# A first stage that runs from a table of ranks: a newly searched table, with new duration figures and new filler matmuls

## The reference, cut to what matters

```python
x = x + _L0_xattn_ref(_layernorm(x), pos, ..., ctx_1024, ...)   # the first stage
x = x + _L0_ffn_ref(_layernorm(x), w1, mean_w1, w2, mean_w2, w3, mean_w3)
```

```python
def _binary_diff_weight(w, base):
    d = w - base
    coeff = jnp.mean(jnp.abs(d))
    return base + coeff * jnp.sign(d)
```

## Time and profile before

| | |
|---|---|
| median of 3 runs | 1187.7 us (1187.0 to 1189.63) |
| the profiled execution, its own time | 1188.86 us |
| its span, first to last instruction | 1187.1 us |
| PE, share of the span | 97% (1157.4 us) |
| DVE, ACT, POOL | 77%, 60%, 39% |
| 0 to 50 us: PE, DVE, ACT busy | 41.91, 38.48, 37.41 us |
| 40 to 360 us: PE, DVE, ACT busy | 303.74, 254.33, 249.23 us |
| 360 to 1187 us: PE, DVE, ACT busy | 820.75, 632.18, 437.06 us |
| granted PE clock, mean of the span | 0.995 |

### The profile page before, as it was taken

One profiled execution on the slowest core, in us unless ns is written; L12 is line 12 of the kernel. 1 busy time (PEld: TensorE's weight loads), 2 busy tenths in 40 slices (PEclk: granted clock), 3 DMA queues, 4 the chain that ended last, 5 costly groups with the idle time before them and its releaser, 6 DMA issues.

```text
span 1187.1 us, 17254 instructions
## 1 busy us (share of the span) xinstructions
PE 1157.4 (97%) x6191; PEld 907.8 (76%) x6191; DVE 917.0 (77%) x1241; ACT 714.0 (60%) x1019; POOL 466.2 (39%) x593
## 2 busy tenths in 40 slices
PE   7998999999999999999999999999999999999998
PEld 5764666667677888888787888888888888888887
DVE  7866688788999788877798678766875777888764
ACT  6878679868686765656556556565663343333342
POOL 3778878886632542435433433354230000000000
PEclk9999999999999999999999999999999999999999
DMA  9677676663513577668766775768667978752232
GB/s 331 222 272 273 232 277 239 256 245 103 178 54 113 180 274 206 216 212 268 235 179 209 267 243 195 241 215 275 200 200 249 344 244 284 258 188 102 94 133 97
DMA packets 99160, 255.39 MB, mean 215 GB/s; under 512 B 9458, under 2 KB 24068, under 8 KB 98820
## 3 DMA queue, kind: packets, MB, share of 16 engines
q1 hardware_dynamic: 95044, 239.62, 56.5%
q0 software_dynamic: 4032, 14.68, 6.9%
HBM read 212.85 MB, written 41.42 MB: 214 GB/s over the span
## 4 chain that ended last, share of the span: by engine, by line
PE 81%; DVE 10%; ACT 4%; issue 3%; DMA 1%; POOL 1%; SPq 0%; DVEq 0%; ACTq 0%; POOLq 0%
PE pair L1590 30%; PE quad L1590 12%; PE quad L1637 11%; PE pair L1637 11%; PE quad L1524 2%; PE quad L1534 2%; PE pair L1571 2%; PE pair L1693 2%; PE pair L1496 1%; DVE negwide L2214 1%; ACT prob L1854 1%; PE pair L1461 1%; PE pair L1476 1%; PE pair L1423 1%; PE quad L1527 1%
## 5 line engine op out<-in xcount | busy, mean ns | idle before, releaser
L2592 POOL TENSOR_TENSOR raw_w<-raw_w,raw_base 128x256 f32<-128x256 f32 x224 | 195.0, 933 | 165.0 <-DMA raw_base<-in_mean_w 165.0
L2125 ACT ACTIVATE split<-grid 128x1024 fp32r<-128x1024 f32 x98 | 104.0, 1061 | 159.8 <-PE pair L1637 147.9
L2534 DVE TENSOR_TENSOR split<-grid,split 128x1024 fp32r<-128x1024 f32 x98 | 119.7, 1224 | 62.1 <-ACT split L2125 61.8
L1637 PE MATMUL quad<-split 128*128 128x512 f32 x588 | 149.3, 389 | 0.5 <-DVE hid L2541 0.5
L1637 PE MATMUL pair<-split 128*128 128x512 f32 x588 | 149.2, 389 | 0.0
L1637 PEld LDWEIGHTS quad<-split 128*128 128x128 f32 x588 | 110.3, 188 | 23.7 <-DVE split L2534 0.9
L1637 PEld LDWEIGHTS pair<-split 128*128 128x128 f32 x588 | 110.4, 188 | 22.9
L1590 PE MATMUL pair<-t_b_hi,ring_hi 128*128 128x512 f32 x224 | 89.0, 397 | 2.5 <-ACT snap L2089 1.8
L2306 DVE TENSOR_TENSOR ring_lo<-raw_base,ring_hi 128x1024 fp32r<-128x1024 f32 x56 | 72.4, 1293 | 22.0 <-ACT ring_hi L2073 14.3
L1590 PE MATMUL pair<-t_b_lo,ring_hi 128*128 128x512 f32 x224 | 88.4, 395 | 0.0
L1590 PE MATMUL pair<-t_b_hi,ring_lo 128*128 128x512 f32 x224 | 87.6, 391 | 0.0
(11 more groups left out here) (328 smaller groups left out, 2801.8 us busy)
## 6 DMA issues: line engine op xcount, KB each, us to landing
raw_w<-in_w SPq DMA_DIRECT2D x56, 512.0 KB, 5.7
raw_base<-in_mean_w SPq DMA_DIRECT2D x56, 512.0 KB, 7.6
grid<-h_blocks SPq DMA_DIRECT2D x49, 512.0 KB, 3.7
late<-in_mean_w SPq DMA_DIRECT2D x28, 512.0 KB, 5.8
late<-in_w POOLq DMA_DIRECT2D x28, 512.0 KB, 5.6
grid<-in_mean_w SPq DMA_DIRECT2D x28, 512.0 KB, 4.8
h_blocks<-work SPq DMA_DIRECT2D x42, 256.0 KB, 3.0
ctxw<-in_w SPq DMA_DIRECT2D x20, 512.0 KB, 4.1
```

Of the source, the lines that this page charges most:

```text
L1637: a = pe.matmul(into[t], found[:, a, t * P:(t + 1) * P], found[:, b, :], start=p == 0 and n == 0 and q < 4, stop=p == PAIRS - 1 and n == 2 ...
L2125: act.activation(splits[n % RINGS][:, 0:2, :], operands(n), ACT.Copy).then_inc(a_hi, 1)
L2534: dve.tensor_tensor(found[:, 2:4, :], operands(n), found[:, 0:2, :].bitcast(F32), ALU.subtract).then_inc(a_lo, 1)
L2592: a = pool.tensor_tensor(w[:, some], w[:, some], base[:, some], ALU.subtract)
```

## The change

It replaces three tables, and no function. `WORK` gets some other figures, `RANK` is replaced as a whole (1019 ranks), `LULLS` has other entries (52 filler matmuls in place of 51). No arithmetic, buffer, DMA or wait of a step is changed; what changes is the order of each engine's list, the banks that steps get, and where the fillers stand.

```diff
-RAT = [... ("DVE", 1.72, 0.2), ("ACT", 0.83), ("DVE", 2.83, 0.25), ("POOL", 2.05), ("POOL", 0.64), ("DVE", 2.2, 2.2)]
+RAT = [... ("DVE", 1.66, 0.2), ("ACT", 0.83), ("DVE", 2.82, 0.25), ("POOL", 1.75), ("POOL", 0.64), ("DVE", 2.42, 2.42)]
...
-    ("measure", 0): (2, 17, 5, 70, 88, 103, ...
+    ("measure", 0): (48, 55, 39, 60, 70, 78, ...
...
-    ('front', 0, 11): (1, 0, ('front', 0, 11)),
+    ('turnmax', 1, 0): (1, 7, ('turnmax', 1, 0)),
-    ('fill', 13, 0): (1, 4, ('turnmax', 5, 0)),
+    ('back', 1, 4): (1, 4, ('weigh', 14, 0)),
-    ('fill', 17, 0): (1, 6, ('weigh', 14, 0)),
+    ('fill', 17, 0): (2, 4, ('weigh', 14, 0)),
+    ('fill', 21, 0): (1, 4, ('front', 6, 15)),
-    ('row', 4, 0): (1, 6, ('back', 1, 19)),
-    ('fill', 33, 0): (2, 6, ('back', 1, 19)),
-    ('back', 4, 4): (1, 6, ('mlp', 0, 0)),
-    ('turnmax', 13, 0): (2, 7, None),
-    ('finish', 6, 2): (2, 6, ('norm', 2, 1)),
-    ('finish', 6, 4): (1, 6, ('norm', 2, 1)),
+    ('turnmax', 11, 0): (3, 4, ('turnmax', 11, 0)),
+    ('fill', 32, 0): (2, 4, ('weigh', 31, 0)),
+    ('finish', 4, 4): (1, 3, ('finish', 5, 0)),
+    ('finish', 5, 4): (1, 2, ('mlp', 25, 0)),
...
```

More of the change, by code:

```diff
@@ L141 @@
     "blend": [("DVE", 0.69, 0.69)] * 4,
-    "norm": [("ACT", 1.24), ("PE", 1.25), ("ACT", 1.01), ("PE", 0.5), ("ACT", 1.05)],
+    "norm": [("ACT", 1.24), ("PE", 1.06), ("ACT", 1.01), ("PE", 0.5), ("ACT", 1.05)],
     "dump": [("SP", 1.65)],
@@ L533 @@
[L533 to L579, removed]
-    ("finish", 16): (704, 809, 875, 900, 926, 927, 964, 995),
-    ("front", 0): (3, 10, 23, 26, 40, 59, 80, 155),
-    ("front", 1): (6, 15, 27, 32, 48, 82, 83, 189),
@@ L614 @@
-    ("norm", 0): (828, 861, 899, 912),
-    ("norm", 1): (829, 897, 920, 922),
-    ("norm", 2): (844, 911, 921, 938),
-    ("norm", 3): (845, 930, 936, 952),
-    ("norm", 4): (853, 931, 945, 953),
-    ("out", 0): (149, 172, 177, 191, 257, 280, 325, 351, 373, 427, 429, 444, 526, 580, 637, 655),
-    ("prep", 0): (814, 827, 857, 1009),
-    ("raw", 0): (752, 816, 841, 848),
-    ("raw", 1): (763, 817, 842, 865),
-    ("raw", 2): (766, 826, 849, 910),
-    ("row", 0): (196, 214, 355, 365, 448, 464, 656, 668),
@@ new lines @@
+    ("blend", 1): (877, 1015),
+    ("blend", 2): (893, 1016),
+    ("blend", 3): (1008, 1017),
+    ("coef", 0): (794,),
+    ("coef", 1): (795,),
+    ("coef", 2): (807,),
+    ("ctx", 0): (372,),
+    ("diag", 0): (8, 137),
+    ("dump", 0): (767, 816, 909, 924, 925, 944, 959, 1014),
+    ("early", 0): (960, 984),
+    ("early", 1): (971, 996),
+    ("early", 2): (972, 1000),
+    ("early", 3): (980, 1007),
+    ("eye", 0): (3,),
+    ("fill", 0): (89, 108, 121, 134, 141, 153, 165, 176, 181, 198, 207, 223, 228, 238, 244, 261, 274, 279, 287, 295, 304,
+        311, 326, 331, 336, 351, 365, 388, 395, 407, 416, 432, 435, 448, 464, 486, 498, 506, 526, 534, 545, 560, 574, 586,
+        599, 604, 625, 632),
@@ new lines @@
+    ("norm", 0): (835, 836, 901, 907),
+    ("norm", 1): (891, 892, 919, 920),
+    ("norm", 2): (905, 906, 923, 932),
+    ("norm", 3): (908, 912, 934, 946),
+    ("norm", 4): (918, 930, 937, 952),
+    ("out", 0): (152, 178, 185, 191, 265, 289, 329, 349, 378, 431, 439, 445, 524, 594, 635, 651),
+    ("prep", 0): (827, 844, 882, 1011),
+    ("raw", 0): (719, 720, 721, 833),
+    ("raw", 1): (732, 799, 843, 852),
+    ("raw", 2): (798, 820, 850, 936),
+    ("row", 0): (196, 219, 353, 373, 446, 461, 652, 669),
@@ new lines @@
+    ("row", 1): (197, 222, 356, 381, 449, 467, 654, 687),
+    ("row", 2): (204, 235, 364, 386, 451, 469, 659, 691),
+    ("row", 3): (206, 250, 366, 387, 456, 477, 660, 692),
+    ("turn", 0): (928, 935, 967, 998),
+    ("turn", 1): (943, 947, 978, 999),
+    ("turn", 2): (964, 988, 989, 1002),
+    ("turn", 3): (954, 968, 981, 1005),
+    ("turn", 4): (965, 994, 997, 1006),
+    ("turn", 5): (987, 995, 1001, 1010),
+    ("turn", 6): (955, 969, 982, 1009),
+    ("turn", 7): (961, 974, 985, 1013),
```

171 lines of the change are left out of this document (97 added, 74 removed).

## The result

Over 22 runs the changed kernel took 1190.7 us by the median (1188.4 to 1196.72), the kernel before, beside it, 1187.57 us (1184.94 to 1189.63). The ratio of the means is 1.0033, interval 1.0026 to 1.0040: it is slower by 0.33%, 3.9 us (the medians differ by 3.1 us). I had forecast 1185.2 us, a gain of 2.5 us. The value lies just inside the upper end of my range, and the kernel moved the other way.

What follows compares the result with a forecast made beforehand. PE's work plus its breaks before the second block's first product was taken to bound the kernel. Terms -1.7 - 1.7 + 1.2 - 0.3 = -2.5 us took the median 1187.7 to 1185.2 us, range 1182.0 to 1191.0.

Steps and rivals of the forecast that it cites:

- What bounds the kernel: Whole kernel: PE's work plus its breaks; a microsecond counts only if the second block's first product starts earlier by it.
- the mark: Start of the second block's first product on PE: 360.2 us before, expected near 357.7.
- Terms B and C: Filler before fill 21; back 7's copy earlier on DVE: each spares PE a fall of the clock, -1.7 us each.
- term A: Head of SP's queue and ACT behind it: measure 0 lands later, delaying front 2's yT; +1.2 us, 0 to +3.3.
- The other moves: Moves elsewhere in the lists: their engines have slack in their stretch of the first 360 us, so taken at nothing.
- rival 1: Clock on PE falls as often as before, here or elsewhere: 1188.6 us, chance 0.20.
- Term E: DVE at 105 us: back 0 steps fill an idle hole, use 15 no longer waits for its fill; -0.3 us.
- Rival 2: Head of the lists: measure 0 lands late in full, everything behind slips by 3.3 us; slower, 1191.0 us, chance 0.20.
- Rival 3: PE in the first 360 us: the new list closes many small unpriced breaks, 3.3 us more gain, 1182.0; chance 0.20.

Runs made afterwards that it cites:

- e12: Changed kernel with the first 150 steps ranked as in the kernel before, banks of the rest held as in the change: ratio 0.9988, 1186.2 us.
- e2: Changed kernel with measure 0's loads first in SP's queue again, as before: ratio 1.0020, mean 1189.8 us.
- e1: Kernel before with measure 0's loads behind measure 2's and the write weights in SP's queue, as changed: ratio 1.0024, mean 1190.1 us.
- e4: Changed kernel with 13 fillers put into PE's wait before front 2 part 11, no order altered: ratio 1.0005, mean 1188.0 us.
- e5: Kernel before with DVE's diag 1 moved behind turnmax 1 part 1, as in the change: ratio 1.0032, mean 1190.5 us.
- e17: e12 with DVE's parts 6 and 8 of back 0 behind back 1 part 1 and use 15, as before: ratio 1.0039, mean 1192.5 us.
- e7: Changed kernel with measure 0's loads first in SP's queue and diag 1 in its old place: ratio 1.0027, mean 1190.1 us.
- e11: Kernel before with 4 fillers before fill 21 and 3 before back 7 part 14, the first in a free bank: ratio 1.0001, 1186.6 us.

## Why the prediction was wrong

**What bounds the kernel** was right, but not the mark that I took for it: the first product of the second block moved by 0.15 us only. Terms B and C behave in the trace as I said; the landing and the `yT` of term A go beyond their bounds. The sum was wrong. In halves, by the means: the head of the lists, in which only term A had a price (+1.2 us), costs 5.1 us (the change against e12); the rest, priced at -3.7, gives 1.1 to 1.4 us (e12 against before).

**Term A (+1.2 us, 0 to +3.3), my whole price of the head, is the step that failed most.** Its chain held link by link: late load, POOL, `yT`. The load landed at 30.8 us, where I took 28.9 and bounded by 30.1; the `yT` started at 38.97 for my 37.7 and bound of 38.9. Two things in it were not as I put them. I gave back 0.9 us for a sum that was only moved; nothing came back, because a second sum, which I had named in the change and left out of the term, stands ahead of the `yn` of `front 3` (e2: 0.9 us late at the first, 1.45 at the second). And I left out what PE does while it waits: 3.59 us of idle time brought the clock down and 1.5 us more. The first fill was 5.0 us late. By e1 the queue alone costs 2.8 us; by e4 fillers in that wait alone give back 3.2 us of the change, so that wait of PE carries much of the loss, the fall behind it some half of the 3.2 us (an estimate by the slopes of the clock loss). The rule of the Trainium skill that I set beside the term (DMA: Bandwidth & Descriptors, section on queues, rings and completion order), that completion need not be in order of issue, does not show here: the second loads of measures 2, 0 and 1 landed in the order of issue, at 21.7, 30.8 and 33.3 us.

**The other moves, taken at nothing, were not nothing.** `diag 1` was among the moves of DVE's list, and I passed over it with the sentence that other steps have slack in their stretch. It had none: 0.32% by e5, some 3 us. I had read the busy shares of 360 us, which say nothing about a stretch of 10. Nor did I see that a step of DVE runs at one speed beside POOL and at another without.

**Terms B and C (-1.7 us each) came true in the profile and hardly in the time.** The new rest of the lists, which holds both and E, gains 1.4 us (e12), not 3.7. The size failed for the reason that rival 1 gave: the clock falls at varying places, and the average run of before has about one fall, where the profile that I priced from had three. All falls of before together are worth about 1.0 us at the end, and the rest of the change brings one of its own, behind the stretch that I had taken as harmless (1.18 us before, 1.50 now). What a fall takes from one product is also not what it takes from the end, by the slope about half. Term E's own sign did not come: `use 15`, at 115.05 us in the trace of the change, still waits for its fill, 0.55 us for 0.33. Its price is open, since e17 could not take it alone.

**The rivals.** Rival 2 was the right one in its direction and in its chain: late landing in full, 1191.0 us, measured 1190.7. I gave it 0.20. That its number fits so well is luck: it slips the first fill by 3.3 us where it slipped by 5.0, it held the clock's falls to be as before, it had no `diag 1` in it, and it left out the gain of the rest. Rival 1's sentence on falls that go elsewhere holds too (1.9 us of clock loss became 4.3). Rival 3 was wrong.

## What to carry to other kernels

Where lists are strict, price a moved step by what is queued behind it on its engine and by the wait that it makes on PE, together with the clock's fall behind that wait; busy shares of a long stretch excuse nothing. A load's place in a queue belongs to the buffer's whole ring: load, difference, sum, next load. And a list that a search made is one piece: exchange it in halves at a clean cut, with the same buffers on both sides, rather than a move at a time. What a fall of the clock is worth is read from many runs: one profile may hold three where the average run has one.

## What the runs showed that I had not expected

In every trace, DVE's TENSOR_TENSOR of 32x512 from two SBUF operands took 0.68 us while POOL was idle and mostly 1.12 us while POOL's differences ran. POOL's differences slow down too: from 0.73 us for one to 1.17 to 1.25 beside `diag 1` in e7, where four took 4.21 us. The Trainium skill (SBUF — State Buffer, section "SBUF: two separate sides") says that DVE operations with two SBUF inputs and GpSimd operations that read SBUF contend for one port pair, which is held for a whole instruction. The traces agree that they slow each other, with these numbers; they do not show who holds what.

The clock's falls came in some runs and not in others of the same kernel, and two groups of fillers in e11 took away nearly all of them, those at a distance too. Why the stretch of 1.76 us at 638 us brings a fall only in some executions is open. Open too is how the head's 5 to 7 us divide among queue, ACT's order and `diag 1`: alone, in the kernel before, queue and `diag 1` cost 2.8 and 3.2 us, while taking both back in the change gave 1.2 us, so that they don't add up. ACT's order was not tried alone.
